# High halves turned on their own semaphore, writes and a load re-placed among the moves, GpSimd's row scaling split around the additions

## The reference

```
x  = layernorm(x + L0(x, adj))     # graph mixing, two linear layers, two batch norms
x1 = x
h  = relu(adj @ relu(adj @ (x1 @ Wg0 + bg0)) @ Wg1 + bg1)
for p in 1, 2, 3, 4:               # an LSTM over windows of p time steps
    h[:, last step of each window] = lstm_last(p, windows of h)
out = layernorm(x1 + h)
```

## Time and profile before

| | us |
|---|---|
| median of 3 runs | 751.12 (750.57 to 752.2) |
| the profiled execution, its time | 748.24 |
| its span, first to last instruction | 746.4 |
| PE busy | 726.6 |
| DVE busy | 644.1 |
| ACT busy | 540.2 |
| POOL busy | 315.2 |

### The profile page before, as it was taken

The page is one execution under the profiler, slowest core; times in us unless marked ns, Lnnn a source line. Parts: engine busy times, 40 slices in busy tenths (PEclk is TensorE's granted clock), DMA queues, the critical chain, the costliest instruction groups (busy, mean ns, idle before and its releaser), DMA issues.

```text
span 746.4 us, 11167 instructions
## 1 busy us (share of the span) xinstructions
PE 726.6 (97%) x3828; PEld 414.8 (56%) x3828; DVE 644.1 (86%) x1379; ACT 540.2 (72%) x882; POOL 315.2 (42%) x289
## 2 busy tenths in 40 slices
PE   8999999999999999998999999999999999999894
PEld 6777544677777776773444444444444444554442
DVE  6888787899998989857998788899998888888987
ACT  4878998567777776748887787777767766676582
POOL 1000000168788787810000001028287385996286
PEclk9999999999999999999999999999999999999998
DMA  5643400024424233113400006051743526519012
GB/s 158 187 139 97 113 1 0 1 62 109 113 58 114 70 101 89 55 29 146 192 1 2 0 11 117 0 101 50 134 109 74 119 51 141 142 28 215 27 57 84
DMA packets 95291, 61.56 MB, mean 82 GB/s; under 512 B 25178, under 2 KB 94212, under 8 KB 94212
## 3 DMA queue, kind: packets, MB, share of 16 engines
q1 hardware_dynamic: 87844, 49.84, 23.7%
q0 software_dynamic: 7392, 11.01, 7.5%
HBM read 27.55 MB, written 16.78 MB: 59 GB/s over the span
## 4 chain that ended last, share of the span: by engine, by line
PE 60%; DVE 21%; ACT 7%; DMA 4%; SPq 3%; issue 3%; POOL 0%; POOLq 0%; DVEq 0%
PE ps L739 8%; PE ps L740 8%; PE ps L748 8%; PE ps L707 7%; PE ps L744 5%; PE ps L753 5%; PE ps L745 5%; ACT work L979 4%; PE ps L646 4%; DVE ln_stats L1263 3%; SPq L510 3%; DVE work L1227 2%; DVE store L1291 2%; DVE ring L1244 2%; DVE ring L1280 2%
## 5 line engine op out<-in xcount | busy, mean ns | idle before, releaser
L979 ACT ACTIVATE work<-ps,gate_bias 128x512 f32<-128x512 f32 x449 | 280.9, 679 | 78.7 <-PE ps L753 44.8
L739 PE MATMUL ps<-store,wih 128*128 128x512 f16 (+1 forms) x443 | 166.9, 377 | 2.4 <-ACT work L979 2.3
L740 PE MATMUL ps<-store,wih 128*128 128x512 f16 (+1 forms) x443 | 166.8, 377 | 0.0
L748 PE MATMUL ps<-store,wih 128*128 128x512 f16 (+1 forms) x443 | 156.2, 377 | 0.0
L577 POOL TENSOR_SCALAR ring<-ring,ln_mv 128x128 f32<-128x128 f32 x112 | 112.8, 1018 | 2.8 <-POOL ln_mv L565 2.7
L1227 DVE TENSOR_TENSOR work<-work 128x512 f32<-128x512 f32 (+1 forms) x129 | 88.2, 684 | 22.0 <-ACT work L986 21.9
L986 ACT ACTIVATE work<-store 128x512 f32<-128x512 f32 x97 | 60.5, 624 | 56.3 <-DVE store L1220 41.2
L588 POOL DMA_DIRECT2D ring<-turned x8 | 10.6, 1319 | 198.5 <-DMA turned<-store 190.5
L744 PE MATMUL ps<-store,whh 128*128 128x512 f16 (+1 forms) x248 | 93.3, 376 | 0.0
L745 PE MATMUL ps<-store,whh 128*128 128x512 f16 (+1 forms) x248 | 93.2, 376 | 0.0
L753 PE MATMUL ps<-store,whh 128*128 128x512 f16 (+1 forms) x248 | 93.1, 376 | 0.0
(11 more groups left out here) (140 smaller groups left out, 1274.0 us busy)
## 6 DMA issues: line engine op xcount, KB each, us to landing
ring<-in_x_dram SPq DMA_DIRECT2D x32, 256.0 KB, 2.9
ring<-in_x_dram SPq DMA_DIRECT2D x16, 512.0 KB, 5.2
x_scratch<-ring SPq DMA_DIRECT2D x16, 512.0 KB, 3.5
ring<-turned POOLq DMA_DIRECT2D x8, 768.0 KB, 6.3
ring<-x_scratch SPq DMA_DIRECT2D x5, 1024.0 KB, 6.4
store<-turned POOLq DMA_DIRECT2D x6, 768.0 KB, 6.8
out_dram<-ring SPq DMA_DIRECT2D x5, 768.0 KB, 3.9
store<-x_scratch SPq DMA_DIRECT2D x3, 1024.0 KB, 14.2
```

What stands on the lines that cost most here:

```text
L739: nc.tensor.matmul(acc(j), w_hi, x_hi, start=True, stop=False)
L740: nc.tensor.matmul(acc(j), w_lo, x_hi, start=False, stop=False)
L748: last = nc.tensor.matmul(acc(j), weights(wih, j)[0], x_lo, start=False, stop=u.first)
L979: nc.scalar.activation(acts[:, n % 2, gate, 0:u.cols], ps[:, gate_bank(q), 0:u.cols], ACT.Tanh if gate == G else ACT.Sigmoid, bias=gate_bi ...
```

## The change

`move_rows` waits for `hi_done` before the four high transposes and for `lo_done` only before the four low ones; of the additions before, the high group waits for the high one of the tile before and the low group for the low one.

SP's order becomes moves 0, 1, 2, W(0,0), move 3, W(1,0), move 4, W(2,0), move 5, W(3,0), W(0,3), load 6, W(4,0), **W(1,3), load 7, move 6**, W(5,0) and the rest in the old order. The loads of tiles 6 and 7 also wait for both additions of tile 5 (`h_added` at 32 * 6).

POOL issues the high addition at the slot where both stood and the low one a slot later. Scaling is cut into powers (`raise_rows`) and rows r (`scale_row`, four instructions), with r = 1 and 2 of a (tile, 0) piece one and three slots after the power if the next tile is moved. That alters POOL's order in two places. Around tile 1 it becomes high addition of 1, power and r = 0 of (0,0), low addition of 1, r = 1, r = 2. Around tile 6 it becomes power, r = 0 and r = 1 of (5,0), high addition of 6, r = 2, low addition of 6.

```
-OUT_DELAY = 4
+def scale_slots():
+    parts = {}
+    for n in sorted(MOMENTS):
+        for piece in MOMENTS[n]:
+            if piece in POOLED:
+                for k, r in enumerate(moment_rows(piece)):
+                    later = (0, 1, 3)[k] if piece[0] + 1 in MOVED else 0
+                    parts.setdefault(n + later, []).append((piece, r))
+    return parts
+
+def write_slots():
+    slots = {}
+    move_of = {tile: n for n in MOVES for tile in MOVES[n]}
+    for n in sorted(MOMENTS):
+        for tile, r in MOMENTS[n]:
+            at = n + (3 if r == 3 else 4)
+            if r == 0 and move_of.get(tile + 2, at) <= n + 7:
+                at = max(at, move_of.get(tile + 2, at))
+            slots.setdefault(at, []).append((tile, r))
+    return slots
...
             def move_rows(tile):
                 n = MOVE_ORDER.index(tile)
-                sp.wait_ge(lo_done, halves_through(max(NUMBER[v] for v in sources(Unit(4, tile, 0)))))
-                wait(sp, h_added, 32 * n)
-                for s in range(2):
+                for s, done in enumerate((hi_done, lo_done)):
+                    sp.wait_ge(done, halves_through(max(NUMBER[v] for v in sources(Unit(4, tile, 0)))))
+                    wait(sp, h_added, 16 * (2 * n - 1 + s) if n else 0)
                     for m in range(CB):
...
                 if piece[1] == 3 and tile + X1_RING < TILES:
                     sp.wait_ge(out_written[tile % X1_RING], 32 * (tile // X1_RING + 1))
+                    sp.wait_ge(h_added, 32 * (len(MOVED) - 1))
                     load_x1(tile + X1_RING)
-            for n in range(N_EARLY, len(UNITS) + OUT_DELAY):
+            for n in range(N_EARLY, max(WRITES) + 1):
                 for tile in MOVES.get(n, ()):
                     move_rows(tile)
-                for piece in MOMENTS.get(n - OUT_DELAY, ()):
+                for piece in WRITES.get(n, ()):
                     write_rows(piece)
...
             for n in range(N_EARLY, len(UNITS)):
                 for tile in LANDS.get(n, ()):
-                    add_rows(tile)
+                    add_rows(tile, 0)
+                for tile in LANDS.get(n - 1, ()):
+                    add_rows(tile, 1)
+                for piece, r in PARTS.get(n, ()):
+                    if piece not in MOMENTS.get(n, ()):
+                        scale_row(piece, r)
                 for piece in MOMENTS.get(n, ()):
-                    scale_rows(piece)
+                    raise_rows(piece)
+                    for part, r in PARTS.get(n, ()):
+                        if part == piece:
+                            scale_row(piece, r)
```

More of the change, by code:

```diff
@@ L215 @@
 TAIL = MOMENTS[len(UNITS) - 1]
+def scale_slots():
[17 more added lines that the diff above has]
+    return slots
 def moment_rows(piece):
     return range(0, 3) if piece[1] == 0 else range(3, 4)
+PARTS, WRITES = scale_slots(), write_slots()
 def resnorm_gnn_kernel(nc, x, adj, W1, b1, g1, be1, W2, b2, g2, be2,
@@ L579, in _, with add_rows @@
                 last.then_inc(x1_ready, 1)
-            def add_rows(tile):
+            def add_rows(tile, s):
                 n = MOVE_ORDER.index(tile)
@@ L584, in add_rows, with raise_rows @@
                 pool.wait_ge(x1_loaded[tile % X1_RING], 16 * (tile // X1_RING + 1))
[L585 to L590, removed]
+                pool.wait_ge(h_moved[s], 16 * CB * (n + 1))
+                wait(pool, h_added, 16 * (2 * n + s))
+                nc.gpsimd.dma_start(rows, h_rows[:, s, :, :].rearrange("p (m r) d -> p m (r d)", r=3),
+                                    accum_op=ALU.add).then_inc(h_added, 16)
+            def raise_rows(piece):
                 n = MOMENT_ORDER.index(piece)
@@ L597, in scale_rows, with scale_row @@
                     .then_inc(end_rstd, 1)
-                if piece in BY_VECTOR:
-                    return
+                if piece in BY_SCALARE:
+                    pool.wait_ge(end_step, 4 * (n + 1))
+                    pool.wait_ge(end_rstd, n + 1)
+                    nc.gpsimd.tensor_tensor(mv[:, 2, cols], mv[:, 1, cols], mv[:, 4, cols], ALU.mult)\
+                        .then_inc(end_offset, 1)
+            def scale_row(piece, r):
+                n, tile = MOMENT_ORDER.index(piece), piece[0]
+                mv = end_mv[:, tile, :, :]
@@ L600, in scale_rows @@
                 pool.wait_ge(end_step, 4 * (n + 1))
                 pool.wait_ge(end_rstd, n + 1)
[L602 to L611, removed]
@@ L612, in scale_rows @@
-                last.then_inc(end_scaled, 1)
+                for m in range(CB):
+                    row = x1_tile[tile % X1_RING][:, 4 * m + r, :]
+                    k = r * CB + m
+                    last = nc.gpsimd.tensor_scalar(row, row, mv[:, 1, k:k + 1], mv[:, 4, k:k + 1],
+                                                   ALU.subtract, ALU.mult)
+                if r == moment_rows(piece).stop - 1:
+                    last.then_inc(end_scaled, 1)
             for n in range(N_EARLY, len(UNITS)):
```

## The result

The changed kernel takes 746.14 us (median of 6 runs, 745.92 to 746.52) against 750.85 us for the kernel before (6 runs, 749.05 to 752.79): a ratio of 0.994, 95% interval 0.9924 to 0.9956, or 4.7 us.

A forecast was written before the change was run, and what follows sets the result against it. PE was taken to bound the kernel, busy except for a 2.30 us wait at (4,3). Removing it, all else costing 0, gave 748.24 - 2.30 = 745.94 for the profiled execution and 751.12 - 2.30 = 748.8 for the median, range 747.2 to 751.4.

The forecast's parts named there:

- The path from tile 6's low addition over DVE to PE's wait at (4,3): Late landing idles DVE 2.86 us before (6,0), delaying `hidden` of unit 121; PE waits 2.30 us, which the change removes.
- no wait in its place: At (4,3), `hidden` of unit 121 ends at 699.26, 0.6 us before PE is ready, so PE doesn't wait.
- the shift to the last instruction: Behind (4,3), ACT follows PE and DVE follows ACT, so the 2.30 us shift stays to the last unit.
- the price of 2.4 us put on W(5,0): Beside tile 6's low addition, this write costs 2.4 us in proportion to its size, so landing takes 8.7 us.
- the rule of turns: DMA engines alternate between software and hardware queues; beside W(5,0), tile 6's low addition would land 3.9 us late, at 686.7.
- Rival B: Load 7 in front of move 6 delays its transposes behind a slow W(1,3) landing: slower, 753.7 us; chance 0.09.
- Rival D: Waits hidden by the modelled ends go too, another 1 to 2 us: 747.3 us; chance 0.06.
- PE's busy time leaves no room for them: Argument against another 1 to 2 us of gain from hidden waits: PE is busy 726.6 of 746.4 us.
- The median stands 2.88 above it: The profiled execution's forecast of 745.94 us is carried to the median by adding 2.88 us, giving 748.8.
- That removes the 0.2 and 1.1 us of DVE, which PE did not wait for: 0.: Tiles 2 to 5 land sooner as moves 2, 4, 5 leave their writes; DVE's waits go, gain 0.
- The forecast hangs on load 7's place more than on the new wait: At move 6, even if the high group still waits for the low half, load 7's place gives the same 748.8.

The follow-up runs named there:

- load7_first_look: One more profile of the kernel before with W(1,3) and load 7 issued ahead of move 6: 747.99 us, span 746.2.
- before_again: The kernel before, unchanged, for a second profile and more times: 750.77 us (12 runs, 748.69 to 752.3), span of the profile 749.0.
- halves_tile6: The kernel before with the new waits of the high and low half for move 6 alone: median 748.54 us, three runs at 745.7 to 746.1.
- w30_behind_move5: The kernel before with W(3,0) issued behind move 5 instead of ahead of it: 747.09 us (11 runs), ratio 0.9961.
- before_look1: The kernel before, unchanged, one more single profile: 750.23 us.
- before_busy: The kernel before with nine dummy matmuls behind unit 122, filling most of PE's wait at (4,3): 748.89 us (12 runs), ratio 0.9988.
- load7_first: The kernel before with W(1,3) and load 7 issued ahead of move 6, old waits and GpSimd order: 746.96 us, ratio 0.9944.
- halves_only: The kernel before with the new `move_rows` alone, high and low group each waiting for its own half: 746.03 us, ratio 0.9929.
- halves_not6: The kernel before with the new waits for moves 0 to 5 alone, move 6 as before: 747.49 us (746.59 to 748.53).
- after_dve_late4: The changed kernel with sixteen more statistics instructions on DVE ahead of the first statistics of (6,0): 750.43 us (12 runs).
- after_dve_late2: The changed kernel with eight more statistics instructions on DVE ahead of the first statistics of (6,0): 747.2 us (746.76 to 747.54).
- pool_only: The kernel before with GpSimd's new order of additions and scales alone: 746.99 us (746.23 to 747.44), ratio 0.9939.
- w30_and_tile6: The kernel before with W(3,0) behind move 5 and the new waits for move 6 alone: 745.98 us, ratio 0.9942.
- after_load7_late: The changed kernel with W(1,3) and load 7 put back behind move 6: 746.05 us (745.9 to 746.1).

## Why the prediction was right in sign and wrong in size

**What held.** The path from tile 6's low addition over DVE to PE's wait at (4,3), the 2.30 us of it, no wait in its place, and the shift to the last instruction: span 744.1 forecast, 744.0 measured. Of the dates, W(1,3) landed when SP was to be free (load 7 out at 655.97 in the new time, 3.7 us ahead of the move; 3.1 forecast), the high addition went out 1.9 us before its forecast, the low one at 676.63 for 676.5. It landed after 5.7 us, not 8.7. That says nothing on the price of 2.4 us put on W(5,0), nor on the rule of turns set beside it (686.7): the write was forecast some 2 us ahead of the addition, went out 4.8 us ahead and had landed 1.1 us after the addition's issue. The nearest figure is a difference between tiles: beside load 6 alone an addition took 9.3 us, beside load 7 and W(5,0) 11.8. Rival B never came near. Rival D had the side of the miss and not the reason: "PE's busy time leaves no room for them" is true of the profiled execution and says nothing of the others, and the waits that went were no hidden ones.

**The step that failed: the executions it was made for.** The sum was made for the profiled execution and carried to the median as a constant ("The median stands 2.88 above it"). The median execution of before has two further costs, each there in some executions and not in others, and the change removes both: the low addition of tile 5 comes too late for PE (2.4 us), and the granted clock falls (1.7 us). The 75 executions of the kernel before that were timed beside the experiments lie like this (median of each group; the clock parts the columns, and a gap in the times parts the rows: none lies between 749.4 and 750.6 at the left, or between 750.7 and 751.8 at the right; that tile 5 is what parts them is inferred from the experiments, as no profile of before lies in the lower row):

| | mean clock 0.994 or more | 0.993 or less |
|---|---|---|
| tile 5 in time for PE | 18 at 748.6 | 14 at 750.2 |
| tile 5 late for PE | 17 at 751.0 | 26 at 752.7 |

The steps are 1.6 and 1.7 us between the columns and 2.4 and 2.5 between the rows, the two prices measured by themselves: 1.7 by a made wait, 2.4 in the profile of `load7_first_look`, with a late tile 5. Of the twelve runs of `before_again`, which are not among the 75, ten fit in and two of 750.8 with a clock of 0.992 and 0.993 lie in the gap at the right; the profiled one of the two had lost 0.6 us before 351. The profiled 748.24 is of the first field. The forecast took off 2.3, which is that field's gain; the median execution pays 4.7.

**The term that was mis-sized.** "That removes the 0.2 and 1.1 us of DVE, which PE did not wait for: 0." In the profiled execution so it was. But the low addition of tile 5 came as the last of a relay: SP issued moves 2, 4 and 5 only behind a write, the write waits for GpSimd's scaling, and GpSimd scales only behind the additions of the move before. Between two executions of one kernel the end of it moved by 2.5 us, 1.2 of them by how fast GpSimd scaled, and DVE's wait with it from 1.1 to 3.6 us (3.9 in `halves_tile6`), beyond what PE could bear. The prediction saw at tile 6 what a load beside a low addition costs and missed the same at tile 5: load 6 went out 1.2 us behind that addition, which took 9.3 us (5.7 in `w30_behind_move5`, where the load went out ahead). Rows 3 showed the wait of 1.1; a wait on a DMA at the end of such a chain has a spread, and it was costed by its one value. And the 1.1 us had a second effect, in the profiled execution as well: without it DVE ends the low half of unit 112 at 662.2 instead of 663.65, and the high one at 659.6 instead of 661.03, so move 6 comes 1.4 us sooner than counted.

**The term that was missing.** The clock. The rows behind PE's wait gave 1.00, so the wait was priced at its own length. In 40 of the 75 executions the mean clock is 0.993 or less, and in the two profiles of before with so low a mean (`before_again`, `before_look1`) it stands at 0.50 or 0.52 for some 3 us behind that wait. That it is always this wait is not shown: one run each of `before_busy` (752.9) and `load7_first` (749.8), whose profiles show no such wait at (4,3), has the low clock too.

**Which part does it.** "The forecast hangs on load 7's place more than on the new wait" was wrong. Load 7's place mends tile 6 and not tile 5; the new waits mend tile 6 and make tile 5 early enough in the five runs of `halves_only`. They alone, or the place of W(3,0) with move 6's new wait, give all of it. GpSimd's order alone gives most of it. They don't add up: the new waits, GpSimd's order and W(3,0)'s place all bring tile 5's relay forward (move 5 starts at 612.52 with the first, at 611.59 with the second), and once both waits are gone PE is busy from 351 to 732 us and nothing is left to gain there.

Open: why GpSimd's scaling of (3,0) takes a microsecond more in some executions, and what delays the high addition behind it. That seven of the eight runs of `halves_not6` lie 0.6 to 1.9 us below its profiled one would follow if tile 5 was on time in them, as in `w30_behind_move5` (747.09, PE's wait 1.8 us); only one profile was taken, so it isn't shown.

## What to carry to other kernels

One profile is one draw. Where the times of the same kernel spread by 0.5% and the profiled execution lies at the edge, the difference between it and the median is made of costs that this profile doesn't show: compare the spread of the times with the price of the waits, and take a second and a third profile before a constant is carried over. A wait of an engine off the critical path that ends on a relay of queues (move behind write behind scaling behind addition) is to be priced by its spread and not by its one value, and a wait of TensorE like this one (2.3 to 2.6 us, with 1.7 more in over half of the executions) by its length and what the clock may take behind it.

## What the runs showed of the hardware

Behind a wait of TensorE of 2.6 us, with every engine at the same work, the granted clock fell to 0.50 in seven of twelve executions and not in five (`after_dve_late4`, by times and mean clocks; one was profiled). Each fall that a profile shows lasted some 3 us and cost 1.6 to 1.7. By the mean clock, the kernels whose profile has a shorter wait there fell less often: none of nine at 0.9 us (`after_dve_late2`), none of six at 1.5 (`pool_only`), one of eleven at 1.8 (`w30_behind_move5`), 40 of 75 at 2.3 to 2.6 (before). The Trainium skill ("TensorE: Matmul & The Clock Gate", section "Part 1: The HAM clock gate (the "warmup" mystery)") tells that a gate passes half of the clock's pulses when the engine has been idle, and that what it goes by runs freely and doesn't start anew with the kernel, so that the moment of a change differs between runs. In this the runs agree: the same wait does it in one execution and not in the next. On how long an idle time it takes, the page and these runs differ, and the measurement decides. A wait of 2.5 us also stands at the end of the kernel, in front of the last turning, where only four transposes are left for TensorE.

An accumulating DMA of 768 KB landed 5.7 to 5.9 us after its issue where the loads and large writes beside it had landed within the first 3 us (low addition of tile 6 in after and `load7_first`, of tile 5 in after, `w30_behind_move5` and `w30_and_tile6`). With a load of 1 MB issued 0.2 to 1.4 us behind it, it took 9.0 to 9.5 (tile 5 in ten profiles, before among them), with that load and W(5,0) behind it 11.3 to 11.9 (tile 6 in eight profiles, before and `after_load7_late` among them), and 7.8 where both had gone out 4 to 4.5 us ahead and landed 2.9 and 4.8 us into it (`halves_only`). So a load that starts with it cost some 3.5 us, and the write some 2 to 2.5 more by the difference. No run has the write beside it without a load for more than the first 1.5 us, so its price alone is not shown.
